# The mask of the decays in attention, written by four products of a quarter of the array

## The reference

```python
    log_f = jax.nn.log_sigmoid(fg)
    cs = jnp.cumsum(log_f, axis=-1)
    diff = cs[..., :, None] - cs[..., None, :]
    mask = jnp.tril(jnp.ones((Sq, Sq), dtype=bool))
    log_D = jnp.where(mask, diff, -jnp.inf) + ig[..., None, :]
    max_log_D = jnp.max(log_D, axis=-1, keepdims=True)
    D = jnp.exp(log_D - max_log_D)
    C = qk * D
    normalizer = jnp.maximum(jnp.abs(C.sum(-1, keepdims=True)), jnp.exp(-max_log_D))
    h = jnp.einsum('bhst,bhtd->bhsd', C / (normalizer + EPS), vh)
```

## Time and profile before

| what | value |
|---|---|
| median of the runs | 3285.47 us (3279.19, 3285.47, 3293.33) |
| profiled execution | 3293.39 us; span from its first to its last instruction 3291.4 us |
| mean granted TensorE clock over the span | 0.972 |
| attention, the first stage | to about 1165 us |
| busy: TensorE, weight loads | 3031.1 us (92%), 2412.8 us (73%) |
| busy: VectorE, ScalarE, GpSimd | 1926.5 us (59%), 1276.7 us (39%), 1043.3 us (32%) |
| mask products (L648), peaks products (L650) in the trace | 128 and 256 records |

### The profile page before, as it was taken

How to read it: one execution, slowest core, us unless ns; L and a number is a source line. 1 busy time by engine, 2 the same in 40 slices (tenths; PEclk the granted TensorE clock), 3 DMA queues, 4 the chain that set the end, 5 groups by cost and what they waited for, 6 DMA issues and landing times.

```text
span 3291.4 us, 60094 instructions
## 1 busy us (share of the span) xinstructions
PE 3031.1 (92%) x23844; PEld 2412.8 (73%) x23972; DVE 1926.5 (59%) x5481; ACT 1276.7 (39%) x2860; POOL 1043.3 (32%) x951
## 2 busy tenths in 40 slices
PE   4888888898888836999999999999999999999998
PEld 3777777777777725777778777778778778777886
DVE  4778888878788766544545554554553554553332
ACT  3688878878788731112112112112112112211210
POOL 3465656656656542111111121111112112112111
PEclk8899999999999958999999999999999999999999
DMA  3133343433433242223223222124222223222211
GB/s 107 53 132 116 118 143 117 139 108 117 138 109 121 88 125 60 40 42 74 38 47 99 35 47 76 33 37 105 42 35 66 55 35 92 57 34 48 59 33 24
DMA packets 140065, 250.67 MB, mean 76 GB/s; under 512 B 31456, under 2 KB 31456, under 8 KB 139784
## 3 DMA queue, kind: packets, MB, share of 16 engines
q1 hardware_dynamic: 106104, 170.80, 15.5%
q0 software_dynamic: 28672, 67.65, 11.7%
q10 hardware_dynamic: 5008, 8.36, 0.8%
HBM read 137.23 MB, written 101.19 MB: 72 GB/s over the span
## 4 chain that ended last, share of the span: by engine, by line
PE 60%; DVE 2%; DMA 1%; issue 0%; POOL 0%; ACT 0%; POOLq 0%; ACTq 0%
PE DN L1485 29%; PE UP L1459 29%; PE TT L1429 2%; DMA w_raw<-in_L_ffn_W_down 1%; DVE c_cand L1171 0%; DVE c_hit L1173 0%; PE c_bank L1165 0%; PE c_bank L1157 0%; DMA xg<-rows_scratch,slots 0%; POOL out_x L1375 0%; ACT z L1401 0%; DVE c_gained L1205 0%; POOL xg L1355 0%; DVE down_lo L1067 0%; DVE c_beyond L1212 0%
## 5 line engine op out<-in xcount | busy, mean ns | idle before, releaser
L1375 POOL DMA_INDIRECT out_x<-y,slots x128 | 201.2, 1572 | 1639.5 <-DVE y L1539 1639.5
L1485 PE MATMUL DN<-down_hi,mid_hi 128*128 128x512 f32 x1408 | 578.8, 411 | 0.0
L1401 ACT ACTIVATE z<-UP,bup 128x512 f32<-128x512 f32 (+1 forms) x352 | 240.7, 686 | 868.9 <-PE UP L1459 857.7
L1459 PE MATMUL UP<-xT_hi,up_hi 128*128 128x512 f32 (+1 forms) x1408 | 553.4, 393 | 3.5 <-ACT z L1401 2.1
L1459 PE MATMUL UP<-xT_hi,up_lo 128*128 128x512 f32 (+1 forms) x1408 | 555.4, 394 | 0.0
L1459 PE MATMUL UP<-xT_lo,up_hi 128*128 128x512 f32 (+1 forms) x1408 | 551.8, 392 | 0.0
L1485 PE MATMUL DN<-down_hi,mid_lo 128*128 128x512 f32 x1280 | 505.0, 395 | 0.0
L1485 PE MATMUL DN<-down_lo,mid_hi 128*128 128x512 f32 x1280 | 504.9, 394 | 0.0
L1515 DVE CAST mid_hi<-z 128x512 fp32r<-128x512 f32 (+1 forms) x352 | 151.6, 431 | 492.4 <-ACT z L1401 492.3
L1384 ACT ACTIVATE xT_hi<-TT 128x512 fp32r<-128x512 f32 x126 | 75.0, 596 | 705.3 <-PE TT L1429 683.2
L1459 PEld LDWEIGHTS UP<-xT_hi,up_hi 128*128 128x128 f32 (+1 forms) x1408 | 260.3, 185 | 69.2 <-ACT z L1401 4.6
(11 more groups left out here) (238 smaller groups left out, 5054.8 us busy)
## 6 DMA issues: line engine op xcount, KB each, us to landing
xs<-in_x SPq DMA_DIRECT2D x32, 1024.0 KB, 7.9
kraw<-in_ctx SPq DMA_DIRECT2D x32, 1024.0 KB, 6.7
out_x<-xs SPq DMA_DIRECT2D x32, 1024.0 KB, 5.7
rows_scratch<-xfb SPq DMA_DIRECT2D x32, 1024.0 KB, 4.3
w_raw<-in_L_ffn_W_down SPq DMA_DIRECT2D x40, 512.0 KB, 4.3
w_raw<-in_L_ffn_W_up SPq DMA_DIRECT2D x16, 682.5 KB, 3.9
mid_hi<-mid_hi ACTq DMA_DIRECT2D x32, 86.0 KB
mid_lo<-mid_hi ACTq DMA_DIRECT2D x32, 84.0 KB
```

The source lines that it names most:

```text
L1375: pool.indirect_dma_start(out_rows, bass.IndirectOffsetOnAxis(ap=slots[:, m:m + 1], axis=0), y[:, t, :], None, compute_op=ALU.add).then_in ...
L1401: act.activation(z[0:r, k % 2, :], UP[k % 3][0:r, :], ACT.Silu, bias=bup[0:r, e // 2, f:f + 1]).then_inc(s["z"], 1)
L1459: mm = pe.matmul(UP[k % 3][0:r, :], weights.up[wa][:, c, f * P:f * P + r], xT[xa][:, c, :], start=first, stop=(c == CH - 1 and wa == 1))
L1485: mm = pe.matmul(DN[m % 2][:, :], lhs, rhs, start=first, stop=(f == FCH - 1 and lhs is parts[-1][0]))
```

## The change

A second mask `maskswap` is made on GpSimd. Its upper 64 partitions hold what the lower 64 of `maskneg` hold, and the reverse. Each bank of `EX` is then written by two products of 64 rows by 64 columns of the array: for the first head of a pair from the upper 64 partitions of both masks, for the second head from the lower 64. The four products of a pair so lie in the four quarters of the array. The peaks products are as before. `skip_group_check` concerns the builder's check of accumulation groups and emits no instruction.

```diff
-        maskneg = sb("maskneg", [P, SEQ], BF16)
+        maskneg = sb("maskneg", [P, SEQ], BF16); maskswap = sb("maskswap", [P, SEQ], BF16)
@@ constants() on GpSimd
                     step(pool.affine_select(out=m, in_=m, compare_op=ALU.is_ge, fill=-BIG, base=0,
                                             pattern=[[0, TILES], [1, P]], channel_multiplier=-1))
+                    step(pool.memset(maskswap[:, :], 0.0))
+                    for half, first in ((slice(0, DH), -DH), (slice(DH, P), 0)):
+                        m = maskswap[half, :].rearrange("p (j s) -> p j s", j=TILES)
+                        step(pool.affine_select(out=m, in_=m, compare_op=ALU.is_ge, fill=-BIG, base=first,
+                                                pattern=[[0, TILES], [1, P]], channel_multiplier=-1))
@@ decays(b, p) on TensorE
+                    top, end = slice(0, DH), slice(DH, P)
+                    for par, r, mask in ((0, top, (maskneg, maskswap)), (1, end, (maskswap, maskneg))):
+                        for t, m in zip((top, end), mask):
+                            pe.matmul(EX[t, par, :], identb[r, r], m[r, :], start=True, stop=False, skip_group_check=True)
                     for par in range(2):
-                        pe.matmul(EX[:, par, :], identb[:, :], maskneg[:, :], start=True, stop=False)
-                    for par in range(2):
-                        pe.matmul(EX[:, par, :], sel[:, 2 * p + par, :], peaks[:, b % 2, :], start=False, stop=True).then_inc(s["ee"], 1)
+                        pe.matmul(EX[:, par, :], sel[:, 2 * p + par, :], peaks[:, b % 2, :], start=False, stop=True, skip_group_check=True).then_inc(s["ee"], 1)
```

## The result

The changed kernel takes 3306.51 us (3304.74 to 3318.14, five executions) against 3285.47: slower by 21.0 us, ratio 1.0066 with a 95% interval of 1.0048 to 1.0084. Its profiled execution took 3310.84 us with a span of 3308.9, so 17.5 us more than the one before.

The account below looks back on a forecast made before the run. The prediction took a TensorE–VectorE loop (turned gates to L606, `rise` to `peaks`) plus TensorE clock falls as the bound; 3293.4 us profiled, +11 direct, +27 for 17 more falls, gave 3331 us, range 3288 to 3354.

Parts of the forecast that it names:

- The forecast mechanism: Around pair 0's wait for the peaks, 0.22 us less streaming and a changed period bring more clock falls; chance 0.50.
- rival (a): Attention stage: clock falls stay as rare as now, only the direct cost counts: 3297 us; chance 0.23.
- full-clock iterations of 34.5 us and a clock of 0.95 or less: Attention stage of the changed profile: about 34.5 us per full-clock iteration, mean granted clock 0.95 or less.
- the direct part: Mask blocks of pairs 1, 2 and 3: 0.13, 0.13 and 0.10 us later, 0.36 an iteration, +11 us over 31 intervals.
- the falls: Attention stage: 22 iterations with a slowed TensorE clock instead of 5, 1.6 us each, +27 us.
- The block of the mask: Pairs 1 and 2, turned k to widths: 0.86 us instead of 0.73; 0.22 saved, two shape changes cost 0.35.
- Rival (b): Quarter products run two by two or one by one: 31 to 71 us more, 3318 to 3375; chance 0.15.
- Rival (c): Pairs 1 to 3: weight loads hide, so shape changes cost under the 0.22 us saved; down to 3266 us; chance 0.12.
- Pairs 1 to 3 on the loop: TensorE to L606, then VectorE from `rise` to `peaks`, bound the iteration, so these pairs' delays count: 0.36 us each iteration.
- Pair 0 and the set-up: Pair 0's block changes by zero, hidden by the 0.75 us wait for `xfT`; extra GpSimd set-up costs nothing.
- The second way to the median: Whole-kernel check: a median run without falls, 3285.5 + 11 + 22 times 1.6, gives 3332 us.
- the choice of 22: Iterations with a clock fall, picked between 5 and 31, nearer the upper end because two stretches differ by 0.01 us.

Follow-up runs that it names:

- e6: Kernel before plus six filling mask products ahead of pair 0's wait for the peaks, and mask products of pairs 1 to 3 issued twice: 3290.0 us, ratio 1.0014.
- e1: Quarter products for pair 0 alone, whole mask products for pairs 1 to 3, otherwise the changed kernel: 3329.5 us, ratio 1.0140 to before.
- e3: The whole change with pair 0's four quarter products issued twice, writing the same values again: 3286.2 us, ratio 0.9999 to before.
- e2: Quarter products for pairs 1 to 3, whole mask products for pair 0, otherwise the changed kernel: 3287.1 us, ratio 1.0005 to before.
- e4: Whole mask products as in the kernel before, plus six filling ones ahead of pair 0's wait for the peaks: 3275.2 us, ratio 0.9968.
- e5: The whole change plus six filling whole mask products ahead of pair 0's wait for the peaks: 3273.0 us, ratio 0.9961 to before.
- e9: Quarter products for pairs 0 and 1, whole mask products for pairs 2 and 3: 3317.3 us, ratio 1.0096 to before.
- e12: Quarter products for pairs 0, 1 and 2, whole mask products for pair 3: 3321.2 us, ratio 1.0100 to before.

## Why the prediction was wrong, point by point

The forecast mechanism, more falls of the clock through less matrix work around pair 0, is the one that was found. The size was wrong: +45 us against +21. The time lies in the stated range, but 3.5 us under the forecast's own (3310 to 3350), and nearer to rival (a)'s 3297 than to 3331. That it lies between the two is no merit of the working. Of the signs, full-clock iterations of 34.5 us and a clock of 0.95 or less did not come true: 34.20 us, and 0.96 from 260 to 1160 us.

In the profiled execution +38 us were forecast and +17.5 came. Of the 20.5 between them 10 are the direct part, 8.5 the falls, and the rest is what lies outside these two terms, above all the 2.7 us by which the part behind the stage became shorter.

**The block of the mask: right.** 0.84 us against 0.86, quarters side by side, two changes of shape dearer than the product saved (in pair 1; pair 2 follows below). Rival (b), quarters one after another, is excluded by their starts. Rival (c), faster, falls with the block: it decided below 0.22 us for the two changes of shape, which cost 0.33.

**Pairs 1 to 3 on the loop: the step that failed.** The prediction said: "A delay counts if it lies on that loop", with the loop from TensorE to L606 and over VectorE's `rise` to `peaks`: +0.36 us an iteration, +11 us. Measured: +0.03, +1 us. Part of the delay is there and arrives at VectorE, as the list of waits of the changed kernel shows:

```profile
DVE rise L916 <- PE T L611: 12.0, 27, 0.5
```

Before it was 9.8 us in 28 waits. In pair 3 the widths come 0.11 us later behind L611, too. This wait is the row that misled me: VectorE does wait there, but what follows has slack. The loop runs past it, which is plain in a view that I had not read for this, ScalarE's timeline. Of the kernel before:

```profile
562.24 0.24 ACT L368 ACTIVATE ll<-vv 128x40 f32<-128x40 f32 x1 [1.43 <-DVE vv L839]
...
574.50 0.40 ACT L470 ACTIVATE T<-fall,prior 128x128 f32<-128x128 f32 x1
```

And of the changed one, where `xfT` follows soon after, for which TensorE waits:

```profile
392.21 0.24 ACT L373 ACTIVATE ll<-vv 128x40 f32<-128x40 f32 x1 [1.33 <-DVE vv L846]
...
404.50 0.40 ACT L475 ACTIVATE T<-fall,prior 128x128 f32<-128x128 f32 x1
...
405.28 0.62 ACT L392 ACTIVATE xfT<-T 128x512 f32<-128x512 f32 x1
```

ScalarE last waits at `ll`, for VectorE. From there it works without a pause, 12.26 us before and 12.29 after, to L470, the one that needs the peaks, and on to `xfT`. The peaks are not what it is late for. One batch earlier in before they end at 538.40 + 1.43 = 539.83, and L470 starts 0.50 us after:

```profile
538.40 1.43 DVE L928 SCALAR_TENSOR_TENSOR peaks<-T,prior,held 32x128 fp32r<-32x128 f32 x4
...
540.33 0.40 ACT L470 ACTIVATE T<-fall,prior 128x128 f32<-128x128 f32 x1
```

In after they end at 404.19, 0.31 us ahead of the 404.50 above:

```profile
402.76 1.43 DVE L935 SCALAR_TENSOR_TENSOR peaks<-T,prior,held 32x128 fp32r<-32x128 f32 x4
```

So of the 0.36 us that were forecast 0.2 reached the peaks, and there they were taken out of a slack of 0.50. And VectorE's `vv` follows from its own statistics, which the masks don't touch. In before:

```profile
552.78 2.47 DVE L789 BATCH_NORM_STATS2 st<-xs 128x6 f32<-128x512 f32 x4
...
559.11 2.47 DVE L789 BATCH_NORM_STATS2 st<-xs 128x6 f32<-128x512 f32 x4
```

In after:

```profile
382.75 2.47 DVE L796 BATCH_NORM_STATS2 st<-xs 128x6 f32<-128x512 f32 x4
...
389.08 2.48 DVE L796 BATCH_NORM_STATS2 st<-xs 128x6 f32<-128x512 f32 x4
```

6.33 us both times, while pair 1's block between them grew by 0.11. So the loop is: TensorE's turned rows, scores and turned gates; VectorE's `tm`, states and statistics; ScalarE from `ll` to `xfT`. TensorE's stretch from pair 1 to pair 3 and VectorE's from `rise` to `peaks` lie beside it, with the 0.75 us of e6: 0.50 at the peaks, and the rest in waits such as that of pair 2 below. Where e6 uses the slack up, the wait appears, in its timeline of ScalarE:

```profile
540.11 0.37 ACT L475 ACTIVATE T<-fall,prior 128x128 f32<-128x128 f32 x1 [0.19 <-DVE peaks L951]
```

Pair 2's own delay hid ahead of that. Its widths wait for ScalarE's `kT`, so that its block, from the end of the turned k to the widths, takes 0.90 us in after and 0.91 before (559.95 to 560.86). The forecast had charged 0.13 us to it. In after the turned k end at 390.03:

```profile
390.30 0.73 PE L657 MATMUL EX<-peaks,sel 128*128 128x512 f32 x2
390.93 0.44 PE L662 MATMUL T<-inner,selP 128*128 128x384 f32 x1
```

**Pair 0 and the set-up: right.** Quarters in pair 0 leave its block as long as it was, as e1 shows. The timeline of TensorE in after answers to the earlier trace rows:

```profile
370.14 0.37 PE L655 MATMUL EX<-maskneg,identb 64*64 64x512 bf16 x1 [1.41 <-DVE peaks L935]
...
371.75 0.65 PE L577 MATMUL T<-ident,xfb 128*128 128x128 f32 x4 [0.54 <-ACT xfT L392]
```

The wait for `xfT`, named as the cover of this block, has shrunk from 0.75 to 0.54 us, and the pause ahead of the masks has grown from about 1.2 to 1.41: the peaks come 0.2 us later. The wait for `xfT` is where the delay that came down from pairs 1 and 3 through the peaks ended. I had charged that delay to the iteration in the same text that named this wait. The first peaks product of the stage starts at 53.67 us, before at 53.75.

**The falls of the clock: mechanism right, size not.** 22 falls were forecast, 21 came. But they were set against 5. The first four intervals were long already (35.39, 37.18, 37.65 and 34.52 us), and I had read only the stretch from 198 us on. Twelve are new, not 17, worth 18.5 us, not 27; the price of 1.6 us each was right. The second way to the median took a median run for one without falls. No run shows that, and the profiled run of e3, at 3285.7 us, has six. The two readings behind the choice of 22 were off as well: the busy 2.33 and 2.34 us of the earlier trace rows leave out the mask product without a record, and 22 itself was a guess between 5 and 31, so that 21 is close to it by luck. The argument that a few tenths of matrix work in the emptiest stretch decide is shown by e1, e2 and e3 together: taking them out of pair 0 alone costs 44 us, out of the other pairs nothing, and putting them back into the whole change as repeated work returns its 21. Rival (a), only the direct part, is excluded by the clock of the stage:

```profile
260.00:560.00 300.00, 270.89 (x4001) 0.97 0.36 123
560.00:860.00 300.00, 274.35 (x4051) 0.95 0.35 119
860.00:1160.00 300.00, 271.33 (x3965) 0.95 0.33 114
```

The same three stretches of before have 1.00, 0.96 and 0.99:

```profile
260.00:560.00 300.00, 264.47 (x4007) 1.00 0.38 128
560.00:860.00 300.00, 267.91 (x3919) 0.96 0.35 118
860.00:1160.00 300.00, 264.25 (x4029) 0.99 0.33 115
```

The Trainium skill ("TensorE: Matmul & The Clock Gate", HAM oscillation) ties the fall to long idle gaps. Here it fell with gaps of 1.2 and 0.75 us as the longest of a steady iteration, and e1, in which neither is longer, fell in every interval. On the gaps of the whole change the prediction was not exact: the one ahead of the masks did grow by 0.2 us, but it is 1.41 us in e2 as well, which is as fast as before.

## What to carry to other kernels

To find whether a delay on an engine counts, follow the loop of one iteration on every engine from its last wait to the first work of the next iteration. A wait of VectorE for TensorE is no proof that TensorE is on it. Where TensorE's clock falls in some iterations and not in others, matrix work around its longest wait is worth more than its own time: taking some out can cost far more than it saves, and work without a result, issued ahead of the wait into a bank that is free (e4, e5), is the cheapest gain here, 0.3 to 0.4%. Once in a row of full shapes, the two changes of shape cost 0.33 us against 0.22 saved; by these two numbers quarters would pay from two such sets in a row on, which is an estimate that no run here shows. And where records of products are missing, a pause is read from the weight load ahead of it too.

## What the runs showed of the hardware that was not expected

Less matrix work made the kernel slower by 44 us, through 0.22 us of streaming an iteration, with no pause longer and no less busy time by the profile (e1). The falls come in series: in e1 all of 31 intervals, in e9 and e12 29, for long stretches alternating between two lengths 0.1 to 0.2 us apart, while e4, with 1.3 us more work in each, has no long one behind the first. And the same quarters that cost 44 us in pair 0 alone cost 21 with those of pairs 1 to 3 beside them.
